# Cross-attention with the next step's query and key-value projections issued in turn

## The reference, cut to what matters

```
def _L0_xattn_ref(latents, context, Wq, Wk, Wv, Wo, q_norm_w, k_norm_w):
    kv = jnp.concatenate([context, latents], axis=1)      # 256 rows
    q = (latents @ Wq)   -> 32 heads of 128
    k = (kv @ Wk), v = (kv @ Wv)   -> 8 heads of 128
    q = rms_norm(q, q_norm_w);  k = rms_norm(k, k_norm_w)
    scores = einsum('bhgqd,bhkd->bhgqk', qg, k) / sqrt(128)
    probs = softmax(scores)
    out = einsum('bhgqk,bhkd->bhgqd', probs, v)
    return out @ Wo
x = x + _L0_xattn_ref(_layernorm(x), ctx, ...)
```

## Time and profile before

| | us |
|---|---|
| Median of 3 runs | 1119.42 |
| Lowest and highest | 1118.90, 1119.43 |
| Span of the profiled execution, first to last instruction | 1116.6 |
| PE busy with matmuls | 1078.4 |
| VectorE busy | 757.3 |
| ScalarE busy | 612.4 |
| GpSimd busy | 360.9 |

### The profile page before, as it was taken

How to read it: one execution, slowest core, us unless ns; L and a number is a source line. 1 busy time by engine, 2 the same in 40 slices (tenths; PEclk the granted TensorE clock), 3 DMA queues, 4 the chain that set the end, 5 groups by cost and what they waited for, 6 DMA issues and landing times.

```text
span 1116.6 us, 19318 instructions
## 1 busy us (share of the span) xinstructions
PE 1078.4 (97%) x6419; PEld 919.2 (82%) x6436; DVE 757.3 (68%) x1561; ACT 612.4 (55%) x2324; POOL 360.9 (32%) x460
## 2 busy tenths in 40 slices
PE   6999999887999999999999999999999999999998
PEld 5677777656888888888888888888888888888886
DVE  6778888865556765675666567566756666667774
ACT  2566666625555555565556555555555555555551
POOL 5622222233115311432332143114312331433443
PEclk8899999998999999999999999999999999999999
DMA  5000010002101100110000011001100110010002
GB/s 180 14 17 9 9 66 10 1 1 95 39 1 58 39 1 2 57 38 0 19 38 38 0 56 38 0 0 56 38 0 0 56 38 0 5 43 1 1 1 76
DMA packets 8935, 31.73 MB, mean 28 GB/s; under 512 B 1600, under 2 KB 1600, under 8 KB 6720
## 3 DMA queue, kind: packets, MB, share of 16 engines
q1 hardware_dynamic: 8896, 31.23, 8.0%
HBM read 29.13 MB, written 2.10 MB: 28 GB/s over the span
## 4 chain that ended last, share of the span: by engine, by line
PE 64%; POOL 7%; DVE 3%; ACT 2%; issue 1%; POOLq 0%; DVEq 0%
PE ps_q L76 15%; PE ps_y L76 14%; PE ps_kv L76 12%; PE ps_s L76 7%; PE ps_o L76 7%; PE ps_pT L1200 4%; POOL wq_lo L866 3%; POOL wkv_lo L866 2%; PE ps_q L1206 2%; PE ps_kv L1211 1%; ACT p L947 1%; DVE neg_max L1032 1%; POOL q_rms L874 1%; POOL k_rms L874 1%; DVE wkv_hi L1025 0%
## 5 line engine op out<-in xcount | busy, mean ns | idle before, releaser
L947 ACT ACTIVATE p<-ps_s,bias,q_rms 128x256 f32<-128x256 f32 x256 | 141.3, 561 | 117.0 <-DVE bias L1036 116.3
L1058 DVE TENSOR_TENSOR pT_lo<-ps_pT,pT_hi 128x512 fp32r<-128x512 f32 x128 | 82.4, 686 | 75.8 <-ACT pT_hi L973 75.6
L983 ACT ACTIVATE oT_hi<-ps_o 128x512 fp32r<-128x512 f32 x64 | 38.3, 598 | 139.2 <-PE ps_o L76 139.2
L872 POOL TENSOR_TENSOR k_rms<-k_mean,rms_eps 128x2 f32<-128x2 f32 x64 | 19.6, 307 | 283.9 <-ACT k_squares L954 283.9
L76 PE MATMUL ps_y<-wo_hi,oT_hi 128*128 128x512 f32 x256 | 106.6, 417 | 0.0
L76 PE MATMUL ps_q<-wq_hi,xT_hi 128*128 128x512 f32 x256 | 101.2, 395 | 2.5 <-POOL wq_lo L866 2.5
L76 PE MATMUL ps_q<-wq_hi,xT_lo 128*128 128x512 f32 x256 | 102.0, 399 | 0.0
L76 PE MATMUL ps_y<-wo_hi,oT_lo 128*128 128x512 f32 x256 | 101.3, 396 | 0.0
L76 PE MATMUL ps_q<-wq_lo,xT_hi 128*128 128x512 f32 x256 | 101.0, 395 | 0.0
L76 PE MATMUL ps_y<-wo_lo,oT_hi 128*128 128x512 f32 x256 | 100.9, 394 | 0.0
L961 ACT ACTIVATE q_sb<-ps_q 128x512 f32<-128x512 f32 x64 | 38.3, 599 | 101.0 <-PE ps_q L76 99.7
(11 more groups left out here) (210 smaller groups left out, 3374.4 us busy)
## 6 DMA issues: line engine op xcount, KB each, us to landing
raw_wq<-in_x_wq SPq DMA_DIRECT2D x8, 1024.0 KB, 4.8
raw_wo<-in_x_wo SPq DMA_DIRECT2D x8, 1024.0 KB, 4.8
raw_wkv<-in_x_wkv SPq DMA_DIRECT2D x8, 512.0 KB, 3.3
ctx_raw<-in_ctxT SPq DMA_DIRECT2D x8, 256.0 KB, 2.6
out<-raw_wq SPq DMA_DIRECT2D x8, 256.0 KB, 2.0
x<-in_x SPq DMA_DIRECT2D x1, 1536.0 KB, 10.8
raw_wq<-in_a_wq SPq DMA_DIRECT2D x2, 512.0 KB, 6.4
raw_wq<-in_a_wo SPq DMA_DIRECT2D x1, 1024.0 KB, 4.8
```

The costliest lines, as they stand in the source:

```text
L947: act.activation(p[:, g, :], ps_s[g // 2][:, g % 2 * KV:(g % 2 + 1) * KV], ACT.Exp, bias=bias[:, g:g + 1], scale=q_rms[:, g:g + 1], accum_ ...
L983: act.activation(oT[0][:], ps_o[:].rearrange("p (g s) -> p g s", g=XG), ACT.Copy).then_inc(o_hi, 1)
L1058: dve.tensor_tensor(pT[1][:, t], ps_pT[t][:].rearrange("p (g s) -> p g s", g=XG), f32(pT[0][:, t]), ALU.subtract).then_inc(pT_lo, 1)
```

## The change

The two functions that project keys and values and queries are replaced by one. It waits for everything that either waited for, then issues one query matmul and two key-value matmuls in turn, twelve times. The six pairs of matmuls from the context come first, then the six from the sequence's own rows. The number of matmuls, their operands and the order of the terms within each of the three sums stay. Both signals are attached at the end: `q_ps` to the last query matmul, `kv_ps` to the last key-value matmul.

```
-            def project_keys_values(s, b, j):
+            def project(s, b, j):
+
                 wait(pe, kT_lo, s)
+                wait(pe, qT_lo, s)
                 if not (isinstance(j, int) and j == 0):
                     pe.wait_ge(wkv_lo, j)
-                rows = slice(b * S, (b + 1) * S)
-                for t, src in enumerate((cT, xT)):
-                    mm = split_matmuls(pe, ps_kv[:, t * NKV:(t + 1) * NKV],
-                                       [(src[0][:, c, rows], src[1][:, c, rows], wkv[0][:, c, :], wkv[1][:, c, :])
-                                        for c in range(C)])
-                mm.then_inc(kv_ps, 1)
-
-            def project_queries(s, b, j):
-                wait(pe, qT_lo, s)
-                if not (isinstance(j, int) and j == 0):
                     pe.wait_ge(wq_lo, j)
                 rows = slice(b * S, (b + 1) * S)
-                split_matmuls(pe, ps_q[:], [(xT[0][:, c, rows], xT[1][:, c, rows], wq[0][:, c, :], wq[1][:, c, :])
-                                            for c in range(C)]).then_inc(q_ps, 1)
+
+                def terms(src, w):
+                    return [(lhsT, rhs) for c in range(C)
+                            for lhsT, rhs in ((src[0][:, c, rows], w[0][:, c, :]), (src[0][:, c, rows], w[1][:, c, :]),
+                                              (src[1][:, c, rows], w[0][:, c, :]))]
+
+                context, own, queries = terms(cT, wkv), terms(xT, wkv), terms(xT, wq)
+                kv = [(ps_kv[:, 0:NKV], i, term) for i, term in enumerate(context)]
+                kv += [(ps_kv[:, NKV:2 * NKV], i, term) for i, term in enumerate(own)]
+                for i, query in enumerate(queries):
+                    q = pe.matmul(ps_q[:], *query, start=i == 0, stop=i == len(queries) - 1)
+                    for out, at, term in kv[2 * i:2 * i + 2]:
+                        mm = pe.matmul(out, *term, start=at == 0, stop=at == len(queries) - 1)
+                q.then_inc(q_ps, 1)
+                mm.then_inc(kv_ps, 1)
...
                     following = j + 1 if b == B - 1 else j
-                    project_keys_values(s + 1, (b + 1) % B, following)
-                    project_queries(s + 1, (b + 1) % B, following)
+                    project(s + 1, (b + 1) % B, following)
```

## The result

The changed kernel takes 1233.46 us (median of 4 runs, 1232.26 to 1234.79), the kernel before 1119.16 us beside it. The ratio is 1.1026, 95% interval [1.1012, 1.1041]: slower by 114.3 us, against a forecast of 123.6. The span of the profiled execution is 1230.2 us, 113.6 more than before.

The account below looks back on a forecast made before the run. PE was taken as the bound, its matmuls filling 97% of the span. Ordinary waits 78.8, changes of head 30.8 and clock 14 us sum to 123.6, which on 1119.4 gives 1243 us; range 1212 to 1270 us.

Parts of the forecast that it names:

- What bounds the kernel, and that the matmuls cost the same: PE, 97% filled, is the bound; the 36 woven matmuls of a step still take 5.68 us, a change of 0.
- slots worse: Rival: alternating width and bank lengthens the woven matmuls' slots by up to 0.56 us a step, 35 us, to 1278; 9%.
- slots better: Rival: woven matmuls speed up by 0.56 us a step while the waits stay, 35 us less, 1208 us; 9%.
- the third rival: The rival of faster woven matmul slots with the waits kept: 35 us below the forecast, 1208 us; 9%.
- The ordinary step: PE waits for copied queries, then keys, as both signals come late: 1.25 us a step, 63 times, 78.8 us.
- T: The moment when ScalarE can start on the query projection's result, 602.96 in the step shown; predicted not to move.
- little for refilling: Allowance for refilling PE's drained array, taking the 1.23 us delay of the key transposes to 1.25 us a step.
- The change of head at full clock: PE idles 4.9 us for wq_lo before the weave; step grows 5.65 us, 4.4 beyond an ordinary one, 30.8 us over seven.
- The clock: PE's clock falls to the 1.2 GHz level in the long wait at each change of head: 2.0 us each, 14 us.
- The rival in which the clock holds: PE's clock keeps its level through the 4.9 us wait at each change of head: 1229 us; 18%.
- hidden after all: Rival: ordinary waits are hidden because engines behind PE run ahead; only the change of head costs, 1173 us; 4%.
- the one on the faster side: Rival: PE's stream speeds up 0.56 us a step and the keys' chain comes free in time, 1108 us; 1%.

## Why the prediction came out as it did

- **What bounds the kernel, and that the matmuls cost the same**: right. A weave of the changed kernel takes 5.65 us where 6.2 would have proved "slots worse" and 5.1 "slots better"; unwoven projections take 5.68. So the weave wins 0.03 us a step, under 2 us in all, where the third rival asked for 35. The kernel with both waits undone says the same, within 0.3% of the one before.
- **The ordinary step**: mechanism right, size 10% too high. Forecast 1.25 us, measured 1.12 (63 times: 70.6 instead of 78.8 us). The mis-sized term is the keys' chain: k_sb starts at T + 1.71, not T + 1.83, because GpSimd's first operation on k_rms lasts 0.19 us instead of 0.31 (its group's mean went from 307 to 194 ns). It now runs when VectorE has nothing to do; before, VectorE was scaling the probabilities beside it. The kernel with four key-value matmuls behind each query matmul and the quarters has both cases in one trace: nine of its operations run beside that scaling and last 0.34 us on average, the 53 that run beside nothing 0.19. So the two go together; no run changed this alone. The two waits of PE, forecast at 0.8 and 0.4 us, were 0.77 and 0.36 by starts. The "little for refilling" in the 1.25 us was not seen: the key transposes start 1.13 us later, and the step grows by 1.12. Nothing behind came late: pT_lo, kT_lo and the scores found their time, as argued.
- **The change of head at full clock**: forecast +5.65 us, measured 18.93 - 13.46 = 5.47 in the kernel with the filled wait. PE started at T + 12.90 instead of T + 13.15, after 4.58 us of idle time instead of 4.9.
- **The clock**: forecast 2.0 us at each change, measured 2.04 on average. The seven intervals are 1.3 to 2.4 us above the 18.93 of the filled wait, so that the mean came so close is in part luck. The rival in which the clock holds is refuted: it fell each time. What was not right is the view that only the long wait counts: in the kernel with only the late signal the clock fell behind an idle time of 1.79 us at four of seven changes. In the changed kernel itself the shorter waits cost nothing of the kind: from the third interval on, its ordinary steps all take 13.98 to 14.22 us.
- **Together**: 70.6 us in the 63 steps, 7 x (20.97 - 13.46 - 1.12) = 44.7 more at the changes of head, and -1.7 outside them make 113.6. The forecast was 78.8 + 44.8. So the difference of 10 us is the ordinary step (8.2 us) and the chance 1.7 us of the start.
- **The rival "hidden after all"** and the one on the faster side ask for an ordinary step near 12.9 us; it is 14.00, forecast "near 14.1".

## What to carry to other kernels

When two results of a saturated engine are interleaved, each is ready only at the end of both; the one with the longer chain behind it should come first, and its slack (here 1.69 us against a signal 2.8 us later) can be read off the timeline before a line is written. The same holds at the input: a wait ahead of an interleaved block is the latest of its waits, so signal and await a weight tile by the pieces in which it is made (in the unwoven kernel this alone was worth 4 us). In a table of waits the larger one need not be the cause: of two waits on one path, only the later sets the time, and moving the larger one away made this kernel 12 us slower.

## What the runs showed of the hardware that was not expected

- TensorE's granted clock fell from 1.00 to 0.50 after an idle time of 1.79 us at four of seven places, when PE had been at work again for 0.3 to 1.2 us; at the other three, with the same wait, it did not, and in the kernel with the old order at the change of head, whose wait is as long (1.76 to 1.80 us), it fell at one of seven, 1.5 us after PE had resumed. After idle times of 4.6 us it fell at all seven places, and after those of 0.8 us in the kernel with the quarters at none.
- Alternating 512- and 256-column matmuls, two PSUM banks and a new stationary operand at each matmul costs nothing: 0.23 and 0.12 us each, as in runs of one width. It gains 0.03 us in 36 matmuls (5.65 us against 5.68): a narrow one right behind a wide one takes 0.118 us on average, where one among narrow ones takes 0.120.
- GpSimd's two-column addition on k_rms takes 0.19 us beside an idle VectorE and 0.31 to 0.34 us in 61 steps of the kernel before and nine of the kernel with the early signal and the quarters, beside VectorE's scaling of the probabilities. That the one makes the other was not tested.
